# A gated cross-attention and FP4 feed-forward block: the low part of q stacked under its high part, and both layer normalisations applied on ScalarE

## The reference

```python
x = x + tanh(g_xattn[0]) * attention(layernorm(x), ctx, ctx, Wq, bq, Wk, bk, Wv, bv, Wo, bo)
x = x + tanh(g_ffn[0]) * ffn(layernorm(x), w_gate, w_up, w_down)

# attention: q = queries @ Wq + bq, 16 heads of 16; scores = q k^T * 16**-0.5; softmax; @ v; @ Wo + bo
# ffn: h = silu(q4(x) @ q4(w_gate).T) * (q4(x) @ q4(w_up).T);  out = q4(h) @ q4(w_down).T
def q4(x):                       # blocks of 16 along the last dimension
    scale = max(max(abs(xb)) / 6.0, 1e-12)
    return GRID[searchsorted(MID, abs(xb / scale))] * sign(xb / scale) * scale
```

## Time and profile before

| | |
|---|---|
| median of 3 runs | 278.96 us (278.86 to 279.12) |
| the profiled execution | 278.86 us |
| its span, first to last instruction | 277.0 us |
| PE busy | 261.6 us (94%), 1657 matmuls |
| PE weight loads busy | 229.2 us (83%) |
| DVE busy | 242.0 us (87%), 713 instructions |
| ACT busy | 165.1 us (60%), 534 instructions |
| POOL busy | 129.7 us (47%), 162 instructions |
| granted PE clock | 1.00 throughout |

### The profile page before, as it was taken

One profiled execution on the slowest core, in us unless ns is written; L12 is line 12 of the kernel. 1 busy time (PEld: TensorE's weight loads), 2 busy tenths in 40 slices (PEclk: granted clock), 3 DMA queues, 4 the chain that ended last, 5 costly groups with the idle time before them and its releaser, 6 DMA issues.

```text
span 277.0 us, 5431 instructions
## 1 busy us (share of the span) xinstructions
PE 261.6 (94%) x1657; PEld 229.2 (83%) x1660; DVE 242.0 (87%) x713; ACT 165.1 (60%) x534; POOL 129.7 (47%) x162
## 2 busy tenths in 40 slices
PE   4999999999999998999999999999999999979795
PEld 2559988999889897999898999999998998757563
DVE  2799999999999998997888889989879999999692
ACT  1438789796765677475665847747576564443421
POOL 1389475823264864641615245354341625543630
PEclk9999999999999999999999999999999999999999
DMA  4993000000000000000000000000000000000001
GB/s 107 311 369 111 1 2 0 0 2 4 2 0 19 2 20 2 20 0 21 1 21 0 0 22 1 19 2 19 0 21 2 22 0 19 2 20 0 19 19 40
DMA packets 9059, 8.64 MB, mean 31 GB/s; under 512 B 1580, under 2 KB 8775, under 8 KB 9031
## 3 DMA queue, kind: packets, MB, share of 16 engines
q1 hardware_dynamic: 7255, 7.50, 8.4%
q10 hardware_dynamic: 1776, 0.79, 1.1%
HBM read 6.19 MB, written 2.10 MB: 30 GB/s over the span
## 4 chain that ended last, share of the span: by engine, by line
PE 46%; issue 21%; POOL 15%; DVE 15%; DMA 2%; SPq 0%; ACT 0%; POOLq 0%; DVEq 0%
PE psT L1963 7%; PE psO L1949 7%; PE psO L1957 7%; POOL ha L1703 4%; POOL hq L1706 4%; PE psG L1935 3%; POOL ha L1714 3%; PE psG L1940 3%; PE psG L1936 3%; PE psO L2018 3%; PE psO L1980 3%; PE psS L1918 2%; PE psS L1915 2%; PE psS L1921 2%; POOL rstd L1675 2%
## 5 line engine op out<-in xcount | busy, mean ns | idle before, releaser
L394 ACT ACTIVATE probs<-psS,negmax 128x77 f32<-128x77 f32 x256 | 59.6, 345 | 4.9 <-DVE negmax L897 4.8
L1957 PE MATMUL psO<-wdT,hT 128*128 128x256 f32 x192 | 44.3, 380 | 1.5 <-ACT hT L445 1.4
L1703 POOL TENSOR_TENSOR ha<-hc,ha 128x704 f32<-128x704 bf16 x15 | 23.2, 1548 | 38.1 <-DVE ha L943 38.1
L1935 PE MATMUL psG<-wgh,xqh 128*128 128x512 f32 (+1 forms) x96 | 38.7, 404 | 2.0 <-DVE h L914 1.5
L1957 PEld LDWEIGHTS psO<-wdT,hT 128*128 128x128 f32 x192 | 35.4, 190 | 6.3 <-issue 1.6
L467 ACT ACTIVATE th<-psG 128x256 f32<-128x256 f32 (+1 forms) x48 | 17.8, 375 | 33.2 <-PE psG L1940 33.1
L1949 PE MATMUL psO<-vblk,pT 128*128 128x51 f32 x320 | 37.5, 271 | 0.0
L421 ACT ACTIVATE pT<-psT 128x512 f32<-128x512 f32 (+1 forms) x48 | 24.6, 530 | 21.5 <-PE psT L1963 21.1
L1949 PEld LDWEIGHTS psO<-vblk,pT 128*128 128x128 f32 x320 | 37.2, 192 | 0.0
L1936 PE MATMUL psG<-wgl,xqh 128*128 128x512 f32 (+1 forms) x96 | 36.0, 375 | 0.0
L897 DVE TENSOR_REDUCE negmax<-psS 128x4 f32<-128x308 f32 x64 | 28.2, 466 | 1.3 <-PE psS L1921 0.8
(11 more groups left out here) (120 smaller groups left out, 609.8 us busy)
## 6 DMA issues: line engine op xcount, KB each, us to landing
out_x<-X SPq DMA_DIRECT2D x16, 128.0 KB, 1.7
X<-in_x SPq DMA_DIRECT2D x2, 512.0 KB, 9.7
wraw<-in_L_ffn_w_down SPq DMA_DIRECT2D x1, 704.0 KB, 9.4
wraw<-in_L_ffn_w_gate ACTq DMA_DIRECT2D x1, 640.0 KB, 9.5
wraw<-in_L_ffn_w_up SPq DMA_DIRECT2D x1, 640.0 KB, 8.4
X<-in_x SPq DMA_DIRECT2D x4, 128.0 KB, 6.5
X<-in_x SPq DMA_DIRECT2D x2, 256.0 KB, 8.8
vblk<-in_vmask SPq DMA_DIRECT2D x2, 255.0 KB, 7.4
```

The costliest lines, as they stand in the source:

```text
L394: ins = act.activation(probs[:, p, hd * S:(hd + 1) * S], psS[g % 2][:, k * S:(k + 1) * S], ACT.Exp, bias=negmax[:, p, hd:hd + 1])
L1703: pool.tensor_tensor(ha[:, p], hc[:, p], ha[:, p], ALU.subtract).then_inc(d_r, 1)
L1935: pe.matmul(o, xqh[:, p, k], wgh[:, k, at:at + w], start=(k == 0), stop=False)
L1957: return pe.matmul(psO[1][:, 0:D], hT[:, p, c * P:(c + 1) * P], wdT[:, c, :], start=(c == first), stop=(c == last))
```

## The change

- **Stacked q.** A group's four heads are 64 of the 128 channels of a chunk; of the others, kh held zeros. Now kh holds each group's keys in both halves, so the 64 idle partitions can carry ql of the same heads. qs[:, p, e, k] has, for the groups of parity e, qh in half e and ql in the other. A group is then qs kh + qs kl, two matmuls (L1988, L1991 of the changed kernel).
- For that the keys must exist twice: `key_weights` (half on DVE, half on ACT) copies Wk into wkd with every 64 columns doubled, `keys_proj` makes 4 x 154 columns where it made 2 x 154, in psT[1] and psS[1], and the key biases, rounding and low parts cover twice the columns. bk is loaded by two DMAs. kmask's pattern repeats every 64 channels.
- **q in two steps.** ACT writes qf = q + bias from PSUM in float32 (two instructions), then casts it to qs's high part (two instructions of 64x256, from SBUF). DVE's subtraction reads qf and the high part from SBUF and writes to the other half of the partitions (two instructions of 64x256 a tile in place of two of 128x128 that read PSUM). psO[0] is free once qf is written (q_f), not once ql is.
- **Normalisation on ACT.** DVE now computes nb = -mean * rstd, 128x1 (`norm_q_bias`, `x1_bias`), and ACT applies scale and bias to 128x256 (`norm_q_apply`, `x1_norm`), for both layer norms of a tile.
- The lists of calls of all engines are rewritten around this, most calls by a place or two. The spins go from 26 matmuls to 24.

```diff
-    kmask = (row[:, None] // HD == np.arange(HPC)[None, :]).astype(np.float32)
+    kmask = (row[:, None] // HD % GH == np.arange(HPC)[None, :] % GH).astype(np.float32)
...
+            def norm_q_apply(n, p):
+
+                done(act, q_nb, 1, n)
+                done(act, q_xnT, 1, n - 2)
+                act.activation(xn[:, p], Xt(n), ACT.Identity, scale=rstd1[:, p:p + 1], bias=nb1[:, p:p + 1]).then_inc(q_xn, 1)
...
             def q_rounded(n, p):
                 if just(n, 0):
                     act.wait_ge(l_bq, 16)
                 done(act, q_q, 1, n)
+                done(act, q_lo, 2, n - 2)
+                for k in range(KC):
+                    act.activation(qf[:, p, k], psO[0][:, k * P:(k + 1) * P], ACT.Identity,
+                                   bias=bqc[:, k:k + 1]).then_inc(q_f, 1)
                 done(act, s_sc, NG, n - 2)
-                for k in range(KC):
-                    act.activation(qh[:, p, k], psO[0][:, k * P:(k + 1) * P], ACT.Identity,
-                                   bias=bqc[:, k:k + 1]).then_inc(q_hi, 1)
+                done(act, q_f, KC, n)
+                for e in range(2):
+                    act.activation(qs[e * H:(e + 1) * H, p, e], qf[e * H:(e + 1) * H, p], ACT.Copy).then_inc(q_hi, 1)
...
+            def key_weights():
+
+                dve.wait_ge(l_wk, 16)
+                dve.tensor_copy(wkd[:, :, :, 0], wk[:, :, :].rearrange("p k (g c) -> p k g c", c=H)).then_inc(s_wkd, 1)
...
-            def norm_q_apply(n, p):
+            def norm_q_bias(n, p):
+
                 done(dve, q_rstd, 1, n)
-                done(dve, q_xnT, 1, n - 2)
-                dve.tensor_scalar(xn[:, p], Xt(n), mv1[:, p, 0:1], rstd1[:, p:p + 1], ALU.subtract,
-                                  ALU.mult).then_inc(q_xn, 1)
+                done(dve, q_xn, 1, n - 2)
+                dve.tensor_scalar(nb1[:, p:p + 1], mv1[:, p, 0:1], rstd1[:, p:p + 1], -1.0, ALU.mult,
+                                  ALU.mult).then_inc(q_nb, 1)
...
+            def q_rest(n, p):
+
+                for e in range(2):
+                    done(dve, q_hi, 2, n, e + 1)
+                    d = (1 - e) * H
+                    dve.tensor_tensor(qs[d:d + H, p, e], qf[e * H:(e + 1) * H, p],
+                                      qs[e * H:(e + 1) * H, p, e].bitcast(F32), ALU.subtract).then_inc(q_lo, 1)
...
             def keys_proj():
                 pe.wait_ge(s_cTs, 1)
-                pe.wait_ge(l_wk, 16)
+                pe.wait_ge(s_wkd, 2)
                 for m in range(KC):
-                    for k in range(KC):
-                        ins = pe.matmul(psT[1][:, m * B * S:(m + 1) * B * S], wk[:, k, m * P:(m + 1) * P],
-                                        ctxT[:, k].rearrange("p b s -> p (b s)"), start=(k == 0), stop=(k == KC - 1))
+                    for e in range(2):
+                        for k in range(KC):
+                            ins = pe.matmul(K_BANKS[m][:, e * B * S:(e + 1) * B * S],
+                                            wkd[:, k, 2 * m + e].rearrange("p d c -> p (d c)"),
+                                            ctxT[:, k].rearrange("p b s -> p (b s)"), start=(k == 0), stop=(k == KC - 1))
...
             def scores(n, p, g):
-                k, at = g // 2, (g % 2) * GW
-                if g % 2 == 0:
-                    done(pe, q_hi, KC, n, k + 1)
+                k, e = g // 2, g % 2
+                if g < 2:
+                    done(pe, q_lo, 2, n, e + 1)
...
-                o, hi, lo = psS[g % 2][:, 0:GW], kh[:, p, k, at:at + GW], kl[:, p, k, at:at + GW]
-                pe.matmul(o, qh[:, p, k], hi, start=True, stop=False)
-                if g % 2 == 0:
-                    done(pe, q_lo, KC, n, k + 1)
-                pe.matmul(o, ql[:, p, k], hi, start=False, stop=False)
+                o, q = psS[e][:, 0:GW], qs[:, p, e, k]
+                pe.matmul(o, q, kh[:, p, k, e * GW:(e + 1) * GW], start=True, stop=False)
...
-                pe.matmul(o, qh[:, p, k], lo, start=False, stop=True).then_inc(s_sc, 1)
+                pe.matmul(o, q, kl[:, p, k, e * GW:(e + 1) * GW], start=False, stop=True).then_inc(s_sc, 1)
```

More of the change, by code:

```diff
@@ L54 @@
 HPC = P // HD
+H = P // 2
 GH = 4
@@ L102, in build @@
         vblk = sb("vblk", [P, B, SC, SLOTS * VW])
+        wkd = sb("wkd", [P, KC, 2 * KC, 2, H])
         wq = sb("wq", [P, KC, D])
@@ L336, in _ @@
         def _(act):
-            act.dma_start(bkc[:, :], bk.rearrange("(k p) -> p k", p=P), allow_slow_non_contiguous=True).then_inc(l_bk, 16)
+            for d in range(2):
+                act.dma_start(bkc[d * H:(d + 1) * H, :, :], bk.rearrange("(k h p) -> p k h", h=2, p=H),
+                              allow_slow_non_contiguous=True).then_inc(l_bk, 16)
             act.dma_start(kmask[:, :], kmask_c).then_inc(l_kmask, 16)
@@ L344, in _ @@
             act.dma_start(bo_b[:, :], bo.rearrange("(a d) -> a d", a=1).to_broadcast([P, D])).then_inc(l_bo, 16)
+            def key_weights():
+                act.wait_ge(l_wk, 16)
+                act.activation(wkd[:, :, :, 1], wk[:, :, :].rearrange("p k (g c) -> p k g c", c=H), ACT.Copy).then_inc(s_wkd, 1)
             def gate_tanh():
@@ L403, in xn_out, with x1_norm @@
                 act.activation(xnT[:, p], psT[1][:, 0:KC * P], ACT.Copy).then_inc(q_xnTs, 1)
+            def norm_q_apply(n, p):
+                done(act, q_nb, 1, n)
+                done(act, q_xnT, 1, n - 2)
+                act.activation(xn[:, p], Xt(n), ACT.Identity, scale=rstd1[:, p:p + 1], bias=nb1[:, p:p + 1]).then_inc(q_xn, 1)
+            def x1_norm(n, p):
+                done(act, b_nb, 1, n)
+                done(act, b_a, 1, n - 1)
+                act.activation(xn2[:, :], Xt(n), ACT.Identity, scale=rstd2[:, p:p + 1], bias=nb2[:, p:p + 1]).then_inc(b_xn, 1)
             def q_rounded(n, p):
@@ L1491, in _ @@
             hidden(9, 1, 0)
+            gated(9, 1, 1)
+            maxima(13, 1, 2)
             maxima(13, 1, 3)
-            gated(9, 1, 1)
+            x_add(10)
+            x_max(11)
             hidden(9, 1, 1)
+            x_sub(10)
+            x_quant(10, 0)
+            gated(9, 1, 2)
             h_max(9, 1, 0)
+            hidden(9, 1, 2)
             h_max(9, 1, 1)
-            gated(9, 1, 2)
-            hidden(9, 1, 2)
-            x_quant(10, 0)
-            x_max(11)
-            x_scale(11)
-            x_inv(11)
             h_max(9, 1, 2)
-            x1_sum(12, 0)
             h_scale(9, 1)
             h_inv(9, 1)
+            x1_sum(12, 0)
             x1_stats(12, 0)
@@ L1594, in _ @@
             x_scale(14)
+            x_inv(14)
             x1_sum(15, 1)
@@ L1609, in _ @@
             gated(13, 1, 1)
-            hidden(13, 1, 1)
             x_add(14)
             x_sub(14)
+            hidden(13, 1, 1)
+            x_quant(14, 0)
+            h_max(13, 1, 1)
+            x_scale(15)
+            x_inv(15)
             gated(13, 1, 2)
-            x_quant(14, 0)
-            x_scale(15)
-            h_max(13, 1, 1)
-            x_inv(15)
             x_a(15)
@@ L1976, in q_proj @@
                 done(pe, q_xnTs, 1, n)
-                free(pe, (b_x1, 1, n - 3, 1), (q_lo, KC, n - 1, KC))
+                free(pe, (b_x1, 1, n - 3, 1), (q_f, KC, n - 1, KC))
                 for m in range(KC):
@@ L2015, in attention_out @@
                 done(pe, b_atTs, 1, n)
-                free(pe, (q_lo, KC, n + 2, KC), (b_x1, 1, n - 1, 1))
+                free(pe, (q_f, KC, n + 2, KC), (b_x1, 1, n - 1, 1))
                 for k in range(KC):
@@ L2249, in _ @@
             attention_out(7, 1)
+            down_all(3, 1)
             xn_T(10, 0)
-            down_all(3, 1)
-            q_proj(10, 0)
+            scores(9, 1, 0)
+            scores(9, 1, 1)
             probs_T(8, 0, 1)
@@ L2293, in _ @@
             down_all(5, 1)
+            scores(11, 1, 3)
             probs_T(10, 0, 1)
@@ L2329, in _ @@
             hidden_T(7, 1, 1)
+            scores(13, 1, 0)
             scores(13, 1, 1)
@@ L2334, in _ @@
             probs_T(12, 0, 2)
-            scores(13, 1, 2)
             q_proj(14, 0)
@@ L2359, in _ @@
             gate_up(10, 0, 0)
-            scores(14, 0, 2)
-            scores(14, 0, 3)
             att_T(13, 1)
             probs_T(14, 0, 0)
+            scores(14, 0, 2)
             gate_up(10, 0, 1)
@@ L2368, in _ @@
             attention_out(13, 1)
+            scores(14, 0, 3)
             down_all(9, 1)
             probs_T(14, 0, 1)
+            probs_T(14, 0, 2)
             scores(15, 1, 0)
             scores(15, 1, 1)
-            probs_T(14, 0, 2)
             x_T(11, 1)
@@ L2378, in _ @@
             gate_up(11, 1, 1)
+            scores(15, 1, 2)
+            scores(15, 1, 3)
             att_T(14, 0)
             probs_T(15, 1, 0)
-            scores(15, 1, 2)
-            scores(15, 1, 3)
             gate_up(11, 1, 2)
```

980 lines of the change are left out of this document (505 added, 475 removed).

## The result

| | before | after |
|---|---|---|
| median | 279.04 us (278.86 to 279.27) | 289.53 us (288.38 to 292.27, 4 runs) |
| ratio, 95% interval | | 1.039 (1.032 to 1.046) |
| profiled execution's span | 277.0 us | 287.9 us |
| first gate matmul | 62.45 us | 79.35 us |
| last tile's first gate matmul | 255.2 us | 266.2 us |

The kernel became 3.9% slower; forecast were 274.8 us and a range of 271.5 to 278.2. The last two rows of the table divide the 10.9 us of span: +16.9 before the first gate matmul, -5.9 between the first and the last tile's gate, nothing behind it (21.8 and 21.7 us).

The account below looks back on a forecast made before the run. PE was taken to bound the kernel from 60 to 235 us, DVE from 20 to 50. 278.86 - 7.2 (scores) + 2.9 (keys) + 0 (DVE) + 1.0 (ACT) - 0.8 (middle) = 274.8 us, range 271.5 to 278.2.

Parts of the forecast that it names:

- the keys: At the head, weight copies and 16 key matmuls instead of 8 move DVE's key bias from 8.37 to near 11.3: +2.9 us.
- Rival 4: The clock falls while PE waits for the first scores; worth at most 1 us, inside the range; no chance given.
- ACT up to 60 us: Early tiles: normalisations and casts add some 5.3 us to ACT, of which +1.0 us was counted (bounds 0 to 5.3).
- DVE up to 50 us: Early tiles: DVE's added key and q work against seven removed normalisations, net +0.2 us, counted as 0.
- Rival 2: The start in series: early tiles wait for each extra hop between engines, +2.8 us in all, 281.7 us; chance 8%.
- I am wrong if the first gate matmul comes later than 69 us: Sign for Rival 2 at the end of the start; the first gate matmul was expected 2 to 4 us after 62.45.
- anyway: First tile: the longer q chain is not covered, but DVE's two weight-scale blocks stand ahead of the subtraction; nothing was counted.
- -7.2: Scores on PE after 50 us: 51 groups each lose one matmul of 0.141 us, 7.2 us off the path.
- -0.8: Middle: normalisations moved to ACT no longer stretch on DVE and make PE wait, 0.8 us less.
- under 500: Sign in the profile after: the subtraction of q's low part (L1062) has a mean under 500 ns.
- the small figure: Middle: subtractions reading two SBUF tensors cost DVE 2.1 us, 0 on the path, against 22 by the strict rule.
- Rival 3: DVE takes PE's place: port stalls on 64 instructions lose 19 us, 3 to 4 reach PE, 277.5 to 278.5; chance 12%.

Follow-up runs that it names:

- e1: The changed kernel with 16 more pairs of matmuls of zeros filling PE's three longest waits at the start: 284.5 us, ratio 1.0175.
- f1_dve6: e3 with the q normalisation of tiles 0 to 5 back on DVE as one operation: three executions at 289.13 to 289.19 us, one at 282.28.
- c1: The kernel before with three more unread ACT operations in each of tiles 0 to 5: 288.39 us, ratio 1.031.
- e4: The changed kernel with both e1's extra matmuls and e3's reordering of DVE's calls: 283.48 us, ratio 1.0131.
- c2: The kernel before with two more unread DVE copies in each of tiles 0 to 5: 286.51 us, ratio 1.0243.
- e3: The changed kernel with q's first subtraction ahead of DVE's second weight-scale block and the gate bias back in its old place: 281.96 us, ratio 1.0101.
- h1: e4 with the second copy of the key weights on DVE instead of ACT: 283.71 us (282.17 to 284.98).
- b_two: The kernel before without its third score matmul, so one small term is left out of the scores: 273.48 us, ratio 0.9772.
- f1_dve6x_sp: f1_dve6 with the x1 normalisation of all tiles also on DVE, plus e1's extra matmuls: 287.54 us, ratio 1.0291.

## Why the prediction was wrong, point by point

**What failed is the start.** Its sum had +3.9 us there (2.9 for the keys, 0 for DVE, 1.0 for ACT); the first gate matmul came 16.9 later. Three sentences carry that:

- *Rival 4, the clock, "worth at most 1 us, inside the range".* It was worth 5.0 us of time by e1, and 6.9 between two executions of f1_dve6. The argument was that the clock had been 1.00 in every stretch; but that was a record of a PE that hardly waited, in a kernel that spends eight pairs of spins on it. The changed one makes PE wait 4.59 us before 14.86. The prediction named the mechanism and never asked how long PE would now be idle, though it had the pieces: four key biases, one step more between rstd and xn, and ACT's queue ahead of it.
- *"ACT up to 60 us: I take +1.0, near the lower end, because 5.4 us of ACT are free in that stretch".* Free time summed over a stretch is not free time where it is wanted. c1 shows it: 7.8 us of ACT work that nobody waits for cost 10.4 at the gate, at least 5.2 of it beside the clock, although ACT was busy only 42.0 of 62.4 us. Sizes were off as well: 0.49 and 0.44 us where the xc row gave 0.31, and some 10 us added where 5.3 was the upper bound.
- *"DVE up to 50 us: I take 0".* It was +5.9 us of busy time up to the gate in e4: the gate bias stretched from 0.34 to 2.0, the subtractions (0.87 a tile for 0.60 where nothing stretched them), the keys. DVE had been called full there, so each microsecond should have been carried over to the end at or near full price: c2's 7.6 us cost 7.6, 4.2 or more of them beside the clock.

Rival 2, "the start in series", with its sign "I am wrong if the first gate matmul comes later than 69 us", is what happened: 79.4. Its 281.7 us is near e3 (281.96), which has another order and some low clock; with the clock held and the order left it is 284.5 (e1). The 1.2 us a tile that it reckoned is near the 1.1 found between tile 0 and 4. Its 8% was far too little, and rivals 2 and 4 were treated as if only one could come, while the waits of one bring on the other.

Two things in the order were put at nothing. The subtraction of tile 0 was said to stand behind DVE's two weight-scale blocks "anyway"; moved ahead of the second (e3), it let the first score start at 21.8 for 23.6. And the tanh of the gates, moved to the head of ACT's list, was not seen at all; it cost nothing in the profiled execution after and about 1 us in e4's.

**The keys.** DVE's bias at 9.87 us, not 11.3: 16 matmuls took 2.35 us because the price of 0.26 was read from eight that by their spacing ran at the lower clock. The copy was dearer than thought (first key matmul 7.50, not 6.8). In h1, where the key matmuls began 0.9 us earlier, no gain showed at the end, within a spread of 2.8 us.

**The middle was right in its mechanism and a third too large.** -7.2 and -0.8 were forecast, -5.9 measured between the gates. The 128 score matmuls are there, PE waits for nothing over 0.6 us from 80 to 245 us, and the subtraction's mean is 506 ns, just over the "under 500" of the sign. The term that was mis-sized is 51 x 0.141: 44 groups lie behind the first gate, and one is worth 0.10 to 0.11. The 0.8 for all else is near the 1.1 us between b_two and the kernel after. In the new order the move to ACT is needed for it (5.4 us by f1_dve6x_sp), in the old one it is not.

**The side of DVE and POOL.** The prediction weighed a rule that names instructions with two SBUF inputs, and took the small figure for the middle. That held there: behind the first tile three subtractions took 0.67 to 0.84 us and the others 0.42. In the first tile it did not: 2.49 us for a pair at 23.14, just where PE waited. Rival 3 reckoned with 64 such instructions; there are 32 (L1062, x32), so that its 19 us should read 10, which DVE's 14.5 us of room would have held.

## What to carry to other kernels

While a pipeline fills, every in-order engine that feeds the first big consumer is on the path: sum each one's busy time up to that consumer's first instruction, and price what a change adds there near its full length, even for an engine that is two thirds busy, until a run shows less. In a rewritten list look for calls that wait for a DMA: what stands behind them waits too. Ask of each longer wait of PE in the start whether the clock was being kept up by hand (here by eight pairs of spins), and lengthen the filling with the wait. Time won in the steady part is small beside both: 5.9 us against 16.9.
